# Transformer kernel on one core: the loads of the exponential stack behind the next unit's high-part writes in SP's order

## What is computed

```python
x = L0_attn_x
xn = _layernorm(x, axis=-1)
x = x + _L0_attn_ref(xn, ...) + _L0_ffn_ref(xn, ...)

# the encoder, L = 4 layers, H = 16 heads of 8 columns, F = 512
for i in range(L):
    xn = layer_norm(x, ln1_w[i], ln1_b[i])
    x = x + mha(xn, mask, in_proj_w[i], in_proj_b[i], out_proj_w[i], out_proj_b[i])   # mask: causal plus alibi
    xn = layer_norm(x, ln2_w[i], ln2_b[i])
    h = jax.nn.gelu(xn @ ffn1_w[i].T + ffn1_b[i], approximate=False)
    x = x + (h @ ffn2_w[i].T + ffn2_b[i])
return layer_norm(x, final_w, final_b)
```

## Time and profile before

| what | value |
|---|---|
| median of three runs | 1693.17 us (1691.81 to 1693.47) |
| the profiled execution, its own time | 1682.76 us |
| its span, first to last instruction | 1680.9 us |
| mean granted clock of TensorE | 0.966 |
| busy: PE, DVE, ACT, POOL | 1426.3, 1130.3, 1224.1, 622.8 us |
| the chain that ended last: PE, DMA, DVE, issue, SP's queue | 36%, 19%, 17%, 15%, 6% |
| SP's hardware queue: bytes, share of 16 engines' span | 150.45 MB, 35.7% |
| POOL's software queue: bytes, share | 36.74 MB, 8.0% |

### The profile page before, as it was taken

How to read it: one execution, slowest core, us unless ns; L and a number is a source line. 1 busy time by engine, 2 the same in 40 slices (tenths; PEclk the granted TensorE clock), 3 DMA queues, 4 the chain that set the end, 5 groups by cost and what they waited for, 6 DMA issues and landing times.

```text
span 1680.9 us, 38344 instructions
## 1 busy us (share of the span) xinstructions
PE 1426.3 (85%) x10656; PEld 943.5 (56%) x10720; DVE 1130.3 (67%) x2851; ACT 1224.1 (73%) x2165; POOL 622.8 (37%) x1052
## 2 busy tenths in 40 slices
PE   0677777479999999999999999999999989899995
PEld 0445544246666666666666665666666655566663
DVE  6577766257766676666776666777666667777762
ACT  3233333158888888888888888888888888888884
POOL 5233332224333333333333333333333335455543
PEclk9699999689999999999999999999999999999997
DMA  3333332254554444555544454444454444444430
GB/s 106 95 114 95 99 108 82 58 131 115 124 122 113 116 123 127 133 119 118 117 113 113 113 120 130 113 116 119 117 119 119 113 130 120 119 119 122 129 94 10
DMA packets 134765, 187.61 MB, mean 112 GB/s; under 512 B 19912, under 2 KB 110696, under 8 KB 134696
## 3 DMA queue, kind: packets, MB, share of 16 engines
q1 hardware_dynamic: 119880, 150.45, 35.7%
q0 software_dynamic: 14848, 36.74, 8.0%
HBM read 120.87 MB, written 65.01 MB: 111 GB/s over the span
## 4 chain that ended last, share of the span: by engine, by line
PE 36%; DMA 19%; DVE 17%; issue 15%; SPq 6%; POOL 2%; DVEq 1%; ACT 1%; POOLq 0%; ACTq 0%
DMA blocks<-split_L 16%; PE pvp L973 8%; PE mxp L917 7%; DVE negm L692 7%; PE exp_ps L950 5%; PE dense L862 4%; PE mxp L921 3%; DVE xn L660 3%; SPq L361 3%; PE dense L991 2%; SPq L385 2%; PE dense L890 2%; PE dense L1003 2%; DVE stats L646 1%; DVE negt L732 1%
## 5 line engine op out<-in xcount | busy, mean ns | idle before, releaser
L825 ACT ACTIVATE probs<-exp_ps 128x512 f32<-128x512 f32 x896 | 525.8, 593 | 322.6 <-PE exp_ps L950 321.1
L692 DVE TENSOR_REDUCE negm<-mxp 128x2 f32<-128x512 f32 x896 | 568.9, 681 | 136.2 <-remote 87.1
L917 PE MATMUL mxp<-blocks,qst 104*128 104x512 f32 x768 | 328.3, 457 | 70.3 <-DMA blocks<-split_L 55.0
L950 PE MATMUL exp_ps<-qbd_l,kst_l 128*128 128x512 f32 x768 | 368.9, 496 | 8.6 <-issue 4.7
L849 ACT ACTIVATE exp_ps<-masktf 128x512 f32<-128x512 f32 x513 | 308.8, 602 | 23.1 <-DVE rest L760 7.0
L492 POOL TENSOR_SCALAR veps<-mv 128x2 f32<-128x2 f32 x144 | 31.7, 220 | 591.9 <-DVE mv L651 588.2
L921 PE MATMUL mxp<-maskb,identb 128*128 128x256 bf16 (+1 forms) x704 | 223.0, 317 | 0.0
L917 PEld LDWEIGHTS mxp<-blocks,qst 104*128 104x128 f32 x768 | 149.5, 195 | 127.5 <-issue 47.8
L973 PE MATMUL pvp<-probs,vst_l 128*32 128x256 f32 (+1 forms) x4096 | 194.4, 330 | 0.6 <-ACT probs L825 0.6
L738 DVE COPY ost<-pvp 128x512 f32<-128x512 f32 x80 | 55.3, 692 | 201.6 <-PE pvp L973 201.6
L950 PEld LDWEIGHTS exp_ps<-qbd_l,kst_l 128*128 128x128 f32 x768 | 144.5, 195 | 41.2 <-issue 31.6
(11 more groups left out here) (95 smaller groups left out, 1995.1 us busy)
## 6 DMA issues: line engine op xcount, KB each, us to landing
split_L<-hi SPq DMA_DIRECT2D x256, 128.0 KB, 2.1
qst<-split_L SPq DMA_DIRECT2D x64, 384.0 KB
kst_l<-split_L SPq DMA_DIRECT2D x64, 384.0 KB
qbd_l<-split_L SPq DMA_DIRECT2D x256, 96.0 KB
split_L<-lo POOLq DMA_DIRECT2D x128, 128.0 KB, 2.1
blocks<-split_L SPq DMA_DIRECT2D x128, 96.0 KB
blocks<-split_L POOLq DMA_DIRECT2D x128, 96.0 KB, 4.1
split_F<-hi SPq DMA_DIRECT2D x64, 128.0 KB, 2.1
```

The costliest lines, as they stand in the source:

```text
L692: dve.tensor_reduce(negm[:, s, qt, h0:h0 + count], mxp[:, (plan.max_chunks * g + ch) % 3, :].rearrange("p (h t) -> p h t", h=count), AX.X, ...
L825: act.activation(probs[:, g[0], ch, :], exp_ps[:, (plan.exp_chunks * g[0] + ch) % 2, :], ACT.Exp, scale=plan.scale).then_inc(q.b_exp, 1)
L917: pe.matmul(mxp[:, bank, :], qst[0:BIAS_END, g[0], qt * P:(qt + 1) * P], kbd[0:BIAS_END, g[0], first:first + count, 0:keys], start=True, s ...
L950: pe.matmul(exp_ps[:, bank, :], kst[plan.name][:, s, g[0], kt * P:(kt + 1) * P], rhs, start=not on_diagonal, stop=True, skip_group_check=T ...
```

## The change

The step `stack+` of unit s + 1 stood behind `op` in the encoder's list, and stands behind `qk+` of unit s + 2 after it. No other engine than SP does anything in this step in the encoder.

```diff
@@ -88,9 +88,9 @@
                 + exps[2:3] + maxes[0:2] + at("xt", s + 2)
-                + exps[3:4] + maxes[2:4] + at("xt+", s + 2) + at("op", s - 1) + at("stack+", s + 1)
+                + exps[3:4] + maxes[2:4] + at("xt+", s + 2) + at("op", s - 1)
                 + exps[4:5] + maxes[4:5] + at("op+", s - 1) + at("qk", s + 2)
-                + exps[5:6] + maxes[5:7] + at("qk+", s + 2)
+                + exps[5:6] + maxes[5:7] + at("qk+", s + 2) + at("stack+", s + 1)
                 + exps[6:7] + maxes[7:9] + at("xn2", s - 1) + end
```

## The result

The changed kernel took 1759.76 us (median of four runs, 1754.70 to 1763.65) beside 1692.49 us for the kernel before: a ratio of 1.040, 95% interval 1.036 to 1.044. It is slower, as forecast, but by 67 us and not by 27, outside the range.

The account below looks back on a forecast made before the run. Bound: the encoder's closed loop through SP's issue order to the blocks load. 1.08 - 0.35 - 0.2 = 0.53 us a slot, 49 slots, 26 us, plus 1 us at layer weights: 27 on 1693.2, forecast 1720 us, range 1698 to 1750.

Parts of the forecast that it names:

- The loop and SP's issue time: Encoder loop on SP: negt issued at H + 6.52 instead of 5.44 (H: high parts' issue), costing 1.08 us a slot.
- Relief of the blocks load: Blocks load, no longer trailed by the stack's loads, lands sooner after its last issue: 0.35 us a slot gained.
- What leads the load: Stack loads now ahead of the maxima's loads, POOL's quarter starting earlier: together -0.2 us a slot, bounds -0.9 and +0.5.
- The exponentials: Before PE's first exponentials: stack lands at H + 9.0 (H: high parts' issue) against a start at 8.20; PE stalls 0.8 us.
- my signs of being wrong: Negt still at H + 5.5; blocks under 3.6 us after last issue; maxima wait gone or exponentials' wait over 1.5 us.
- The stall is covered by the longer wait for the blocks: PE before the maxima: arrival at H + 13.2, blocks awaited until about H + 13.7, so the 0.8 us stall costs nothing.
- The first slots: Encoder's first slots: no separate stall term, counted among the 49 slots at 0.53 us each.
- The last layer: Last layer's 12 slots: negt ready only at H + 6.37, issue cost 0.15 us each minus equal relief, total 0.
- Rival 3: Exponentials' stack becomes the bound if landing over 3.0 us after last issue; at 3.8, 0.8 us a slot more, 1760; chance 0.05.

Follow-up runs that it names:

- up to three late loads: None, two or three qbd stack loads moved behind the high parts, against the kernel before; 1690.3, 1671.9 and 1677.4 us.
- two and three late loads: Only two or three of the five stack loads (qbd) moved behind the high parts, against the kernel before; ratios 0.992 and 0.993.
- issues without bytes: Kernel before, stack loaded where it was, plus five 8-column loads behind three waits at the new place; 1764.8 us, ratio 1.048.
- the attempt: Kernel before with two qbd loads moved behind the high parts and negt issued by POOL in all layers but the last; 1753.8 us, ratio 1.037.

## Why the prediction was right in sign and wrong in size

- **The loop and SP's issue time**: right for negt. It was issued at H + 6.52 (median), as forecast; 5.44 is where it stood with up to three late loads.
- **Relief of the blocks load**: the landing was near the forecast, by two errors that cancel. 4.68 us from the last issue to the maxima were to become 4.13. The 4.22 measured looks like a hit, but it is PE's arrival; the load itself landed 0.68 us sooner after its last issue (4.48 to 3.80), where relief and new neighbours were to give 0.55. The last issue in turn ended 1.46 us later than before (H + 8.42 to 9.88) and not 1.08. Together (medians do not add up exactly) the blocks came 0.67 us later, H + 13.71, where I had 0.53 and H + 13.7. With two and three late loads, where SP's issues of negt, qst and blocks stood where they were, the relief was 0.3 us, the size read from the six undisturbed slots. The Trainium skill, DMA: Bandwidth & Descriptors, section "Queues, rings and completion order", says that each DMA engine consumes the descriptors of a ring in order. By my reading of it there would have been no relief; the 0.3 us speak against that reading.
- **What leads the load**: qst was to be issued at H + 7.5 and came at 7.81, because SP found the low parts not yet landed (H + 7.3, before H + 5.25). I had written "somewhat later" and priced it within 0.45; it was 2 us. This is most of what the last issue was later than forecast.
- **The exponentials: the step that failed.** I took the stack to land 2.5 us after its last issue, at H + 9.0, and PE's stall for 0.8 us. The landing was 3.1 us after (H + 9.6), and I had put no price on negt, which is issued behind it and is waited for as well. By the row of before, 2.2 us from issue to landing and 0.56 to the first exponential, it alone gives H + 9.3. In the changed kernel, right behind the stack, it took 3.2 us (median slot), and the start was at H + 10.17. PE's wait was 2 us and not 0.8. Of my signs of being wrong the last one came true: the wait in front of the maxima gone in most slots and over 1.5 us in front of the exponentials.
- **"The stall is covered by the longer wait for the blocks"**: just about so, where the clock held. PE reached the maxima at H + 13.9 in those 33 slots against the 13.7 forecast, and the slots grew by 0.69 us against 0.53. But this cover left nothing in reserve, and the stall counted for more than its length: some 20 us of the loss are the clock's. No term of the sum looked at the clock, and no rival did. In the undisturbed slots of this kernel the late blocks (H + 13.7) alone would have cost nearly as much as PE's late arrival; that the late start of the exponentials suffices is shown by the runs in which the blocks landed at H + 13.2 (issues without bytes) and H + 12.2 (the attempt) and the loss was much the same.
- **The first slots** were priced like the others, some 2 us for four of them; with what is ahead of them they cost 11.0.
- **The last layer** was put at nothing. Its slots grew from 20.6 to 21.1 us (median). Negt's issue time did not change much (H + 6.3 to 6.7), as forecast, but its landing did (8.5 to 9.8), and the first exponentials moved from H + 8.9 to 10.1. The last fifteen slots cost 11.8 us.
- **Rival 3**, the exponentials' stack as the bound, decided at 3.0 us after its last issue, was the nearest to what happened, and had a chance of 0.05, too low, because I judged it by a stack that landed alone. That its price, 1760 us, is the measured time is luck: it has a stack that lands 3.8 us after its last issue, where 3.1 was measured, and nothing for negt, the clock and the last layer.

## What to carry to other kernels

A queue that is idle most of the time can still have no room at one place: count the issue times between the event that releases a step and the next event that needs the queue, and move only what fits (here three loads of 0.8 us, not five). A small transfer that a main engine waits for should be issued ahead of the bulk loads of every queue, not only of its own: negt landed in 2.2 us ahead of them and in 3.2 to 4.1 us right behind or beside them. And where a change puts a wait in front of TensorE, price the half clock that may follow it, not the wait alone.

## What the runs showed of the hardware that was not expected

- Negt, 16 KB: 2.2 us from issue to landing when issued 0.6 us ahead of POOL's blocks loads; 3.2 us when 0.6 us behind them, with hardly any bytes ahead in its own queue; 3.2 us right behind the stack in the changed kernel; 4.1 us when POOL issued it together with qst, and 4.0 us in the last layer of the run with negt from POOL, where qst again went out within 0.1 us of it, with the stack ahead as well.
- Of the 44 slots with a wait of some 2 us in front of the exponentials, eleven got 3.4 us at half clock, the others none. The eleven waits were 1.95 to 2.59 us long, the other 33 were 1.40 to 2.25 us, and nine of these were 1.95 us or more, so the length of the wait alone does not pick the slots. What does was not settled; that filling the wait removes the stretches was.
- Five loads of 8 columns took SP 3.87 us to issue, and five of 256 columns 3.61: SP's time goes by the number and form of the loads, hardly by their bytes.
